# Attention slots of a gated block: a constant column for empty masks, the mask in four loads, and other places for the extra work

## What is computed

```python
x = x + tanh(g_xattn[0]) * xattn(layernorm(x), ctx_2048, mask_BxS2_bk0)
x = x + tanh(g_ffn[0])   * ffn(layernorm(x), w_gate, w_up, w_down)

def xattn(h, mem, mask):           # h (32,128,512), mem (32,128,512), mask (32,128)
    scores = einsum('bsd,bmd->bsm', h, mem) / sqrt(512)
    attn = softmax(where(mask[:, None, :], scores, -1e30))
    out = einsum('bsm,bmd->bsd', attn, mem)
    return where(any(mask, -1)[:, None, None], out, 0)   # the valid flag of a batch

def ffn(x, w_gate, w_up, w_down):  # 512 -> 2048 -> 512, all float32
    h = silu(x @ w_gate) * (x @ w_up)
    return keep_2_of_4(h) @ w_down  # in each group of four the two largest by size
```

## Time and profile before

| | |
|---|---|
| median of 3 runs | 1119.65 us |
| the profiled execution | 1116.94 us |
| its span, first to last instruction | 1115.1 us |
| around the span (1116.94 - 1115.1) | 1.8 us |
| busy in the span | PE 97%, DVE 73%, ACT 56%, POOL 19% |
| DMA | 254.75 MB, mean 228 GB/s |
| mean granted TensorE clock | 0.998 |

### The profile page before, as it was taken

One profiled execution on the slowest core, in us unless ns is written; L12 is line 12 of the kernel. 1 busy time (PEld: TensorE's weight loads), 2 busy tenths in 40 slices (PEclk: granted clock), 3 DMA queues, 4 the chain that ended last, 5 costly groups with the idle time before them and its releaser, 6 DMA issues.

```text
span 1115.1 us, 15146 instructions
## 1 busy us (share of the span) xinstructions
PE 1082.4 (97%) x4960; PEld 880.0 (79%) x4960; DVE 809.6 (73%) x1400; ACT 620.1 (56%) x1132; POOL 210.6 (19%) x328
## 2 busy tenths in 40 slices
PE   6998799999999999999999999999999999999998
PEld 5776587777878888888888888888888888888886
DVE  6999969879897757576775767675757565565765
ACT  5999678566765544454544444454445454443452
POOL 5576610121210111111111111001111111111111
PEclk9999999999999999999999999999999999999999
DMA  7899586798869977797779777888878666767726
GB/s 273 295 349 329 202 326 226 219 289 280 257 226 354 356 196 198 187 257 185 202 197 374 182 202 200 237 235 208 231 230 274 151 153 156 189 159 189 199 29 137
DMA packets 89533, 254.75 MB, mean 228 GB/s; under 512 B 9072, under 2 KB 9072, under 8 KB 85104
## 3 DMA queue, kind: packets, MB, share of 16 engines
q1 hardware_dynamic: 67856, 205.55, 52.2%
q0 software_dynamic: 21600, 48.24, 26.1%
HBM read 154.14 MB, written 99.61 MB: 228 GB/s over the span
## 4 chain that ended last, share of the span: by engine, by line
PE 73%; DVE 14%; ACT 4%; issue 4%; POOL 2%; DMA 2%; SPq 0%; DVEq 0%; ACTq 0%; POOLq 0%
PE ps_y L1302 9%; PE ps_a L1231 9%; PE ps_a L1233 9%; PE ps_a L1235 9%; PE ps_y L1304 9%; PE ps_y L1303 9%; PE ps_d L1233 4%; PE ps_d L1231 4%; PE ps_d L1235 4%; PE ps_c L1233 2%; PE ps_c L1231 2%; PE ps_c L1235 2%; DVE beats L980 2%; DMA w_raw<-in_L_ffn_w_up 1%; DVE x1n L930 1%
## 5 line engine op out<-in xcount | busy, mean ns | idle before, releaser
L569 POOL DMA_DIRECT2D out_rows<-y_out x124 | 107.1, 871 | 735.2 <-ACT y_out L717 712.7
L1231 PE MATMUL ps_a<-xm,w_ring 128*128 128x512 f32 x512 | 200.7, 392 | 3.6 <-ACT cp L597 3.3
L1233 PE MATMUL ps_a<-xm,w_ring 128*128 128x512 f32 x512 | 200.3, 391 | 0.0
L1235 PE MATMUL ps_a<-xm,w_ring 128*128 128x512 f32 x512 | 200.2, 391 | 0.0
L1302 PE MATMUL ps_y<-dn,h_hi 128*128 128x512 f32 x480 | 188.9, 394 | 4.4 <-ACT y_out L717 3.3
L1304 PE MATMUL ps_y<-dn,h_lo 128*128 128x512 f32 x480 | 187.4, 390 | 0.0
L1303 PE MATMUL ps_y<-dn,h_hi 128*128 128x512 f32 x480 | 187.0, 390 | 0.0
L717 ACT ACTIVATE y_out<-ps_y,ffn_gate 128x512 f32<-128x512 f32 x124 | 84.8, 686 | 158.4 <-PE ps_y L1304 158.3
L694 ACT ACTIVATE h_hi<-hidden 128x512 fp32r<-128x512 f32 x128 | 73.6, 626 | 107.0 <-DVE hidden L1006 107.0
L980 DVE TENSOR_TENSOR beats<-h_abs 128x512 bf16<-128x512 f32 x186 | 117.7, 684 | 1.3 <-ACT h_abs L687 1.3
L1231 PEld LDWEIGHTS ps_a<-xm,w_ring 128*128 128x128 f32 x512 | 96.4, 188 | 26.2 <-issue 5.2
(11 more groups left out here) (109 smaller groups left out, 1876.6 us busy)
## 6 DMA issues: line engine op xcount, KB each, us to landing
w_ring<-w_scratch SPq DMA_DIRECT2D x147, 512.0 KB, 4.5
...
```

The lines of the kernel that those rows point to most:

```text
L569: nc.gpsimd.dma_start(out[RING * (n // (2 * TILES * QS)) + TILES * ORDER[order] + n % TILES], y_out[:, n % 4], accum_op=ALU.add).then_inc( ...
L1231: nc.tensor.matmul(to, w_ring[:, k, e, 0, c], xm[:, k, 0, c], start=begins and c == 0, stop=False, skip_group_check=not begins)
L1233: nc.tensor.matmul(to, w_ring[:, k, e, 0, c], xm[:, k, 1, c], start=False, stop=False, skip_group_check=not begins)
L1235: last = nc.tensor.matmul(to, w_ring[:, k, e, 1, c], xm[:, k, 0, c], start=False, stop=c == 1, skip_group_check=not begins)
```

## The change

The valid flags go. The row of neg_scores gets a constant 129th element, 0.9e30, set once. A masked score is 1e30 there, so for a batch with no valid entry the least of the row is 0.9e30, and all exponentials become zero; 1e-30 is added to the softmax sum in the operation that adds epsilon, which now spans three columns. The gate alone scales the probabilities. The mask is loaded in four pieces of 128 KB, each behind a pair of inputs, and the conversions move to slots 1, 5, 7 and 10. On POOL neg_mean now stands ahead of the power, and the wait for the softmax sum ahead of base. On DVE the statistics of x_in now stand between x1 and x1n. The tables are new: from slot 3 to 34 each slot has one extra ACT operation except slots 9 to 11, which have a weight sum on DVE; X0_AT of k = 1 begins at 26, not 29; the last two spreads come in 33 and 34 and two sums in 36 and 37. In the first pair x_high_at and x_low_at of points 1 and 3 move behind the copies of the next unit, dn_low and add_c22 go ahead of x_low_at(s, 0), and spread(u+1, 2) goes behind silu1.

```diff
@@ -29 +29 @@
+FEW = 0.9e30
+LEAST = 1e-30
@@ -45,18 +49,18 @@
 X_TO = (0, 1, 5, 3, 4, 2, 6)
 X_AT = {m: i for i, m in enumerate(X_TO)}
-CONVERT = {1: (0,), 2: (1,), 3: (2, 3)}
+CONVERT = {1: 0, 5: 1, 7: 2, 10: 3}
 KEEP = {0: (2, ALU.is_ge, 2.0), 1: (0, ALU.is_ge, 1.0), 2: (1, ALU.is_le, 0.0), 3: (3, ALU.is_le, 1.0)}
 PAIR = {(0, 1): 0, (2, 3): 1, (1, 3): 2, (0, 2): 3, (1, 2): 4, (0, 3): 5}
 ORDER = (1, 0)
-PIECE_AT = {4: (0, 2), 7: (0, 3), 10: (1, 0), 13: (1, 1), 21: (1, 2), 24: (1, 3), 27: (2, 0), 30: (2, 1)}
-SPREAD_AT = {3: (0, 0), 6: (0, 1), 9: (0, 2), 12: (0, 3), 20: (1, 0), 23: (1, 1), 26: (1, 2), 29: (1, 3)}
-SUM_AT = {13: ((0, 0), (0, 1)), 14: ((0, 2),), 15: ((0, 3),), 30: ((1, 0), (1, 1))}
-W0_AT = {5: 0, 8: 1, 14: 2, 15: 3, 16: 4, 17: 5, 18: 6}
-X0_AT = {19 + i: (0, i) for i in range(7)} | {29 + i: (1, i) for i in range(7)}
+PIECE_AT = {4: (0, 2), 5: (0, 3), 8: (1, 0), 9: (1, 1), 18: (1, 2), 19: (1, 3), 34: (2, 0), 35: (2, 1)}
+SPREAD_AT = {3: (0, 0), 4: (0, 1), 6: (0, 2), 7: (0, 3), 17: (1, 0), 18: (1, 1), 33: (1, 2), 34: (1, 3)}
+SUM_AT = {9: (0, 0), 10: (0, 1), 11: (0, 2), 12: (0, 3), 36: (1, 0), 37: (1, 1)}
+W0_AT = {5: 0, 8: 1, 12: 2, 13: 3, 14: 4, 15: 5, 16: 6}
+X0_AT = {19 + i: (0, i) for i in range(7)} | {26 + i: (1, i) for i in range(7)}
...
-        neg_scores = sb("neg_scores", [P, 2, M], F32, 4)
+        neg_scores = sb("neg_scores", [P, 2, M + 1], F32, 4)
...

+            def load_mask(m):
+                at_m = slice(m * GROUP_M, (m + 1) * GROUP_M)
+                sp.dma_start(mask_in[:, at_m], mask.rearrange("b m -> (b m)")[at_m].rearrange("(a n) -> a n", a=1)
+                             .to_broadcast([P, GROUP_M])).then_inc(mask_loaded[m], 16)
...
             for b in range(INPUTS):
                 load(b)
-                if b == 1:
-                    sp.dma_start(mask_in, mask.rearrange("b m -> (b m)").rearrange("(a n) -> a n", a=1)
-                                 .to_broadcast([P, B * M])).then_inc(mask_loaded, 16)
+                if b == 5:
+                    load_w_piece(sp, nc.sync, 0, 0)
+                    load_w_piece(sp, nc.sync, 0, 1)
+                if b == 7:
+                    load_mask(1)
+                if b == 2:
+                    load_mask(0)
                     for n, g in enumerate((g_xattn, g_ffn)):
                         sp.dma_start(gates_in[:, n:n + 1], g.rearrange("(a n) -> a n", a=1)
                                      .to_broadcast([P, 1])).then_inc(gates_loaded, 16)
-            load_w_piece(sp, nc.sync, 0, 0)
-            load_w_piece(sp, nc.sync, 0, 1)
+            load_mask(2)
...
@@ -524,29 +534,28 @@
                     pool.wait_ge(stats1_done, n + 2)
                 if second:
                     pool.wait_ge(stats2_done, n - 5)
-                if first or second:
-                    part_v = slice(0 if first else 1, 2 if second else 1)
-                    nc.gpsimd.tensor_tensor(base3[:, k, part_v], bn_mv[:, k, part_v, 1], eps[:, part_v],
-                                            ALU.add).then_inc(base_done, 1)
-                    pool.wait_ge(base_done, n + 2)
+                part_p = slice(0 if first else 1, 3 if third else 2 if second else 1)
                 if third:
                     pool.wait_ge(probs_done, n - 3)
-                part_p = slice(0 if first else 1, 3 if third else 2 if second else 1)
+                nc.gpsimd.tensor_tensor(base3[:, k, part_p], stats[:, k, part_p, 1], least[:, part_p],
+                                        ALU.add).then_inc(base_done, 1)
+                if first:
+                    nc.gpsimd.tensor_tensor(neg_mean[:, k:k + 1], stats[:, k, 0, 0:1], minus_one[:],
+                                            ALU.mult).then_inc(neg_mean_done, 1)
+                pool.wait_ge(base_done, n + 2)
                 nc.gpsimd.tensor_tensor(power3[:, k, part_p], base3[:, k, part_p], exponent3[:, part_p],
                                         ALU.pow).then_inc(power_done, 1)
                 if first:
-                    nc.gpsimd.tensor_tensor(neg_mean[:, k:k + 1], bn_mv[:, k, 0, 0:1], minus_one[:],
-                                            ALU.mult).then_inc(neg_mean_done, 1)
                     pool.wait_ge(neg_mean_done, n + 2)
                     pool.wait_ge(power_done, n + 2)
                     nc.gpsimd.tensor_tensor(neg_mean_rstd[:, k:k + 1], neg_mean[:, k:k + 1], power3[:, k, 0:1],
                                             ALU.mult).then_inc(shift_done, 1)
                 if n in CONVERT:
-                    pool.wait_ge(mask_loaded, 16)
-                    for at_m in CONVERT[n]:
-                        part_m = slice(at_m * RING * M, (at_m + 1) * RING * M)
-                        nc.gpsimd.tensor_scalar(mask_neg[:, part_m], mask_in[:, part_m], -BIG, BIG, ALU.mult,
-                                                ALU.add).then_inc(mask_neg_done, 1)
+                    m = CONVERT[n]
+                    pool.wait_ge(mask_loaded[m], 16)
+                    part_m = slice(m * GROUP_M, (m + 1) * GROUP_M)
+                    nc.gpsimd.tensor_scalar(mask_neg[:, part_m], mask_in[:, part_m], -BIG, BIG, ALU.mult,
+                                            ALU.add).then_inc(mask_neg_done, 1)
                 if n - 1 in W0_AT:
                     w_low(pool, nc.gpsimd, 0, W0_AT[n - 1])
                 if n - 1 in X0_AT:
@@ -608,8 +617,8 @@
                 if 0 <= b < B:
                     act.wait_ge(neg_max_done, b + 1)
                     wait(act, pT_done, b - 1)
-                    nc.scalar.activation(probs[:, b % 2], neg_scores[:, b % 2], ACT.Exp, bias=neg_max[:, b % RING:b % RING + 1],
-                                         scale=-1.0, accum_out=base3[:, (b + 4) % RING, 2:3]).then_inc(probs_done, 1)
+                    nc.scalar.activation(probs[:, b % 2], neg_scores[:, b % 2, 0:M], ACT.Exp, bias=neg_max[:, b % RING:b % RING + 1],
+                                         scale=-1.0, accum_out=stats[:, (b + 4) % RING, 2, 1:2]).then_inc(probs_done, 1)
...
@@ -640,10 +648,10 @@
                     act.wait_ge(pT_done, b + 1)
                     wait(act, av_done, b - 1)
                     if b == 0:
-                        act.wait_ge(gate_valid_done, 1)
+                        act.wait_ge(gates_done, 1)
                     nc.scalar.activation(probsT[:, b % 2], ps_pT[:, 0:P], ACT.Identity,
-                                         scale=gate_valid[:, b:b + 1]).then_inc(pT_copied, 1)
-                if n == 1:
+                                         scale=xattn_gate[:]).then_inc(pT_copied, 1)
+                if n == 2:
                     act.wait_ge(gates_loaded, 32)
...
@@ -735,6 +743,7 @@
                         spread(act, u + 1, 0)
                     absolute(s - 1, 1, 1)
                     copy_a0(u, 1)
+                    x_high_at(s - 1, 3)
                     absolute(s - 1, 1, 2)
                     absolute(s - 1, 1, 3)
                     if building:
...
@@ -776,7 +785,6 @@
                         if building:
                             for k in ((), (2, 3), (4, 5), (6,))[t]:
                                 w_high(act, u + 1, k)
-                    x_high_at(s, 1)
                 else:
                     w_high(act, 1, 0)
                     w_high(act, 1, 1)
...
@@ -855,10 +863,10 @@
                 copy_d0(u, 1)
                 if building:
                     w_high(act, u + 1, 0)
-                    spread(act, u + 1, 2)
                 silu1(u, 0)
                 silu1(u, 1)
                 if building:
+                    spread(act, u + 1, 2)
                     w_high(act, u + 1, 1)
                     spread(act, u + 1, 3)
                 for j in second:
@@ -876,7 +884,6 @@
                     if building:
                         for k in ((), (2, 3), (4, 5), (6,))[t]:
                             w_high(act, u + 1, k)
-                x_high_at(s, 3)
             for t, tiles in enumerate(((), kept_order(LAST)[:1], kept_order(LAST)[1:], ())):
                 copy_y(LAST, 0, t)
                 if 0 <= b < B:
                     dve.wait_ge(bn2_done, b + 1)
-                    nc.vector.bn_aggr(bn_mv[:, n % RING, 1], bn6[:, 1, b % 2]).then_inc(stats2_done, 1)
+                    nc.vector.bn_aggr(stats[:, n % RING, 1], bn6[:, 1, b % 2]).then_inc(stats2_done, 1)
                 b = n + 1
                 if 0 <= b < B:
                     dve.wait_ge(bn1_done, b + 1)
-                    nc.vector.bn_aggr(bn_mv[:, n % RING, 0], bn6[:, 0, b % 2]).then_inc(stats1_done, 1)
-                if n in CONVERT:
-                    dve.wait_ge(mask_loaded, 16)
-                    for m in CONVERT[n]:
-                        nc.vector.tensor_reduce(valid[:, m * RING:(m + 1) * RING],
-                                                mask_in[:, m * RING * M:(m + 1) * RING * M]
```

(37 more changed lines are left out.)

60 lines of the change are left out of this document (29 added, 31 removed).

## The result

The changed kernel takes **1127.73 us** (median of 5 runs, 1124.68 to 1128.33) against 1119.65 (now five runs, 1117.45 to 1125.32): the ratio is 1.0065, with a 95% interval of 1.0038 to 1.0091. It is slower by some 8 us, where 4.6 us less had been forecast. The profiled execution took 1128.33, its span is 1126.2.

What follows compares the result with a forecast made beforehand. TensorE was taken to bound the kernel from 345 to 1072 us, but not the attention stage before. Terms -2.8 + 2.6 - 1.9 - 2.5 = -4.6 took 1119.65 to 1115.0 us, range 1108.0 to 1121.0.

Steps and rivals of the forecast that it cites:

- First pair: TensorE's 210.8 us before 345 us: fewer waits for copies give 2.5 of 8.55 us idle, -2.5 us.
- Start: Before slot 6: four reductions go and mask loads are split, against a spread moved into slot 4: -2.8 us.
- Slots: Attention slots 6 to 33: 105.2 us instead of 102.6, with 3.96 for each low-operation slot: +2.6 us.
- End of the stage: Attention slots 34 and 35: a subtraction and two x1n collisions go: -1.9 us, between 0.6 and 2.4.
- (a): Attention slots: low operation starts after x1n, 11 slots fall from 3.96 to 3.28: -7.5 us more, 1107.5; chance 0.20.
- (b): Attention slots with low operation and subtraction: power and subtraction delay each other, +4.9 or +4.2 us, 1119.95 or 1119.2; chance 0.25.
- (c): First pair: TensorE's clock falls in the copy_d0 wait of u = 2, -2.5 becomes about +1, 1118.5 us; chance 0.10.

Runs made afterwards that it cites:

- e4: Changed kernel's attention stage, with the kernel before's orders on SyncE, ScalarE and VectorE in the loops over s: 1114.25 us.
- e5: Changed kernel with x_low_at(s, 0) back ahead of both add_c22 and compare(REST[2:]) ahead of dn_low(s - 1) on VectorE: 1118.12 us.
- e10: e5 with, in the first step of each later pair, x_high_at(s, 0) behind dn_high, x_low_at(s, 0) behind gated1, its store behind the seven loads: 1114.72 us.
- e1: Changed kernel with load_dn(s) ahead of the store x_stored_at(s, 3) on SyncE's queue: 1123.61 us.
- e7: e4 with the statistics of x_in behind those of x1, so x1n is ahead of both, as in the kernel before: 1114.48 us.
- e2: Changed kernel with the x_blk load for the next pair but one ahead of the seven 1 MB xm loads: 1127.72 us.
- e3: Changed kernel with the queue edits of e1 and e2 together: 1123.62 us.
- e8: Changed kernel with x1n first in slots without sum or subtraction, and the kernel before's orders from the second pair on: 1114.88 us.

## Why the prediction was wrong

**The step that failed** is a half sentence of the part on the first pair: "SyncE's later store of x_out holds back reload issues by some us, each a whole unit ahead of its use: nothing". It looked at the reloads of w_ring only. The raw down weights stand behind such a store, 7 us later than before (496.57 against 489.73), and ScalarE waits 10.4 us for them in four waits. The first of the seven xm loads waits 6.0 us for the last store instead of 0.5, and x_blk lands behind them with its reader already waiting. With it failed what was not weighed at all: VectorE's block (x_low_at(s, 0) behind add_c22, dn_low ahead of the comparisons), which goes on past 345 us in the steps of pairs 2 and 3 (s from 4 to 11). The first paragraph had said that no edit after 345 us counts unless it starves TensorE, and the working then did not ask of each edit whether it does. Together these cost 15.6 us in the traces and 13.5 by the medians of e4 and the changed kernel, where the sum had 0. e5 shows that the block alone accounts for 9.6 us of the time; e10 shows another 3.4 at the x_blk stall; e1, on top of the changed kernel, 4.1 for the late down weights (in part the same stalls as in e5). How much the changed orders add at the x_blk stall is less sure than the rest, since e7 has that stall with the old orders.

**Part by part**, by the traces:

- *Start*, -2.8 forecast: the first neg_scores is at 13.16 (17.38 before), that of slot 6 at 21.22 (25.46 in the earlier trace rows): -4.2, near the upper end of its bounds.
- *Slots*, +2.6: from slot 6 to 34 it is 104.10 us (125.32 - 21.22) against 102.6: +1.5. The slot with a low operation (3.96), the one without (3.15 in slot 7, 3.09 in slot 18; 3.16 forecast) and the one with a sum (3.69 to 3.74; 3.76 forecast) came nearly as worked out; slots 8 and 19 took 3.39 and 3.38. The low operation was late and harmless in slots 6 and 26, and the x_in load was late in slot 21 (4.72).
- *End of the stage*, -1.9: -1.7 (4.5 at the first product less 2.8 at slot 34).
- *First pair*, -2.5: -0.1. The wait for copy_a0 fell from 1.91 to 0.78, and the wait for copy_d0 of u = 2 came, 5.78 us (some 6 forecast), with half clock behind it. The working took the pair's gain as if it came on top of the earlier start. In e4 the old orders turn a lead of 5.2 into 3.8, and in e7 4.4 into 3.0, while the new ones keep 4.5 at 4.6 in the changed kernel and 5.1 at 5.1 in e2; but in e1 they turn 4.1 into 2.9 and in e3 5.2 into 3.1. So the old orders give back 1.4 and the new ones between nothing and 2.1, and what the new orders are worth in this pair is not clear of that spread. The wait for copy_d0 was mis-sized too: TensorE lost 4.2 us to the last product of u = 2, where 2 had been worked out.

The sum to 349 us was -4.6, as forecast, by luck: two errors cancel (2.4 too little in the attention stage, 2.4 too much in the first pair), and e1 with the same program up to there stood at -2.9.

**The rivals.** (a) *No collision* did not come; e7 shows that its price of 0.68 a slot was right. (b) *Power and subtraction* did not collide in slots 22 to 25 and 29: the power kept 0.85 and the subtraction 0.70 with the power 0.04 ahead. A lead of 0.04 was enough in these; slot 9 of e8 is the case in which the lead was too short:

```profile
31.76 1.40 POOL L546 TENSOR_TENSOR power<-base,exponent 128x3 f32<-128x3 f32 x1
31.77 0.68 DVE L316 TENSOR_TENSOR w_blk<-w_blk 128x512 f32<-128x512 f32 x1
```

With the power 0.01 ahead it took 1.40 all the same, 0.55 more, and the subtraction nothing more. (c) *The first pair gives nothing*, in a clock that falls after copy_d0: that came, and the measured -0.1 lies between its +1 and the -2.5 of the sum; but it ends at 1118.5 and could not give the result.

The rival that was missing is the one of the other sign past 345 us: an operation moved out of an engine's idle time into its chain, step after step.
